# Cross-attention of a two-layer decoder: ScalarE's copies ahead of its newest exponential

## The chip, the cores and the metric

One core of a Trainium2 chip runs the whole program. Its engines are TensorE (PE, with PEld for its weight loads), VectorE (DVE), ScalarE (ACT), GpSimd (POOL) and SyncE (SP, which issues transfers). The time is device microseconds from start to end of one execution; the median of a few runs counts.

## What is computed

A decoder of two layers on x (4, 256, 256) with a context (4, 512, 64), all fp32. Each layer is self-attention, cross-attention and a mixture of experts, each followed by a layer norm of the sum with its input. The change touches cross-attention alone:

```
q_r    = rope((x @ Wq.T per head) @ w_kc_q) @ W_qr     # per head: 64 wide
k_r    = kv_r @ W_kr                                   # kv_r: the rotated context
attn   = softmax(q_r @ k_r.T)                          # 16 heads, 256 x 512 for each of 4 batches
ctx_c  = attn @ kv_r
out    = (ctx_c @ w_kc_kv, heads side by side) @ Wo.T
```

The kernel multiplies the weights together beforehand, so that scores are a query of 64 against the rotated context, and the context product is attn with the 64 columns of the rotated context.

## The kernel before

Cross-attention is cut into UNITS = 128 units per layer. Unit i is one tile of 128 queries of one head: scores of 128 x 512, their exponential, and the product with the context. Four units make a group g = i // 4 (one pair of heads, two query tiles). Every engine has a loop `cross_attention` of its own, written out by hand, over the same counter i; engines work their instructions in this order and meet through semaphores. In iteration i:

- TensorE (lines 654 to 694) makes the scores of unit i (two matmuls, L673 and L674, waiting until the score bank is free: `x_exp` of unit i - 3 in layer 0, which has three score banks, i - 4 in layer 1, which has four), then transposes the probabilities of unit i - 4 (L681, four transposes of 128 x 128 into bank 3 or 4, waiting for `x_nrm`, and for the copy of unit i - 6 out of that bank: `turned_probs_wait`), and, where i % 4 is 1, the context product of group i // 4 - 2 (L692, 16 matmuls).
- VectorE (lines 1147 to 1175) takes the negated row maximum of unit i (L1155, `x_max`), then the reciprocal of the sum of unit i - 2 (L1160, `x_rec`, after `x_exp`), and in layer 1 the copy of the transposed probabilities of an odd unit i - 4 (L1167, `x_tev_d`). In layer 0, for i up to 84, it also does one of five parts of the rounding of expert weights (lines 1171 to 1175).
- GpSimd (lines 1854 to 1862) multiplies the exponentials of unit i with the reciprocal (L1858, `x_nrm`); in layer 0, for i < 80, in iterations with i % 5 of 3 or 4 a part of that rounding (L1868, L1874) comes behind.
- ScalarE (lines 1641 to 1671) takes the exponential of unit i with its row sum (L1656, `x_exp`; a second small instruction reads the accumulator), waiting for `x_max` of unit i and `x_t` of unit i - 6; then copies the transposed probabilities of unit i - 4 out of bank 3 or 4 (L1664, `x_tev_a`), all units in layer 0, the even ones in layer 1; then, where i % 4 is 0, the context of group i // 4 - 3 (L1671, `x_ctx`).

Layer 0 runs as one loop over 128 units with the queries of the second half made in between at i = 64; layer 1 runs as two loops of 64 units. A loop goes on for some iterations behind its last unit, in which only the older units are worked.

Of the kernel before, what the change touches and what calls it, by code (L numbers as in the profile page):

```python
# [22 lines left out]
ACT = mybir.ActivationFunctionType  # L23
# [3 lines left out]
B, S, D = 4, 256, 256  # L27
# [5 lines left out]
NPAIR = H // 2  # L33
# [17 lines left out]
def program(nc, a, out):  # L51

    ctx = ExitStack()
    with ctx:
# [16 lines left out]
        ps = [ctx.enter_context(nc.psum_tensor(f"ps{i}", [P, 512], F32)) for i in range(8)]  # L71

        def sem(name):
            return ctx.enter_context(nc.semaphore(name))

        def at(kb, n, dt=F32, pattern=None, **k):

            words = n if dt != BF16 else n // 2
            v = mem[:, int(kb * 256):int(kb * 256) + words]
            v = v if dt == F32 else v.bitcast(dt)  # L80
            return v.rearrange(pattern, **k) if pattern else v
# [16 lines left out]
        PR = [at(kb, L) for kb in (80, 82, 84, 86, 200, 202)]  # L98
        SB = [[1, 2, 7], [0, 1, 2, 7]]
        CT = [at(kb, NPAIR * B * S, pattern="p (g s) -> p g s", g=NPAIR) for kb in (136, 136)]  # L100
# [5 lines left out]
        def col(n):  # L106
            cols[0] += n
            return small[:, cols[0] - n:cols[0]]
# [3 lines left out]
        nmax, esum, rinv = col(8), col(8), col(8)  # L112
# [36 lines left out]
        x_s, x_max, x_exp, x_nrm = sem("scores"), sem("neg_max"), sem("probs"), sem("probs_normed")  # L149
        x_rec, x_t, x_tev_a, x_tev_d = sem("sum_recip"), sem("probsT_psum"), sem("probsT_even"), sem("probsT_odd")  # L150
        x_pv, x_ctx = sem("context_psum"), sem("context_ready")
# [1437 lines left out]
        def _(act):  # L1589
# [44 lines left out]
            def high_queries(k, bank):  # L1634

                for hh in range(2):
                    r = slice(64 * hh, 64 * hh + 64)
                    last = act.activation(QS[2 * (k % NPAIR) + hh][r, :], ps[bank][r, :], ACT.Copy)  # L1638
                last.then_inc(x_qhi, 1)

            def cross_attention(lay, first, end):
                u0, g0 = UNITS * lay, UNITS // 4 * lay
                for i in range(first, end + 9):
                    if lay == 0 and i % (UNITS // 2) == 0 and i < end:
                        if i:
                            act.wait_ge(x_s, i)
                        for k in range(8 * (2 * i // UNITS), 8 * (2 * i // UNITS) + 8):
                            act.wait_ge(x_q, k + 1)
                            high_queries(k, SB[0][k % 3])
                        if i == 0:  # L1650
                            weights_copied(3, ps[3])
                    if i < end:
                        act.wait_ge(x_max, u0 + i + 1)
                        if i >= 6:
                            act.wait_ge(x_t, u0 + i - 5)
                        act.activation(PR[i % 6], ps[SB[lay][i % len(SB[lay])]][:, :], ACT.Exp, bias=nmax[:, i % 8:i % 8 + 1],  # L1656
                                       accum_out=esum[:, i % 8:i % 8 + 1]).then_inc(x_exp, 1)
                    j = i - 4
                    if first <= j < end and (lay == 0 or j % 2 == 0):
                        g = j // 4  # L1660
                        act.wait_ge(x_t, u0 + j + 1)
                        if g >= 2:
                            act.wait_ge(x_pv, g0 + g - 1)
                        act.activation(PT[g % 2][:, :, j % 2, (j // 2 % 2) * P:(j // 2 % 2 + 1) * P],  # L1664
                                       ps[3 + j % 2][:, :].rearrange("p (k s) -> p k s", k=KC), ACT.Copy)\
                           .then_inc(x_tev_a, 1)
                    g = i // 4 - 3
                    if i % 4 == 0 and first <= 4 * g:
                        b, p = g // NPAIR, g % NPAIR
                        act.wait_ge(x_pv, g0 + g + 1)  # L1670
                        act.activation(CT[lay][:, p, b * S:(b + 1) * S], ps[5 + g % 2][:, 0:S], ACT.Copy).then_inc(x_ctx, 1)  # L1671

            def weights_copied(f, bank):
                act.wait_ge(f_wt, f + 1)
                dst = w13T[:, :, f * 512:(f + 1) * 512] if f < 8 else w2T[:, :, (f - 8) * 512:(f - 7) * 512]
                act.activation(dst, bank[:, :].bitcast(BF16).rearrange("p (c n) -> p c n", c=DC), ACT.Copy).then_inc(f_wt_ev, 1)
# [127 lines left out]
            weights_copied(0, ps[1])  # L1804
            output_and_layernorm(0)
            cross_attention(0, 0, UNITS)
            output_and_layernorm(1)
            experts_layer0()
# [3 lines left out]
            for half in range(2):  # L1812
                narrow_queries(half)
                cross_attention(1, half * UNITS // 2, (half + 1) * UNITS // 2)
# [264 lines left out]
```

## Time and profile before

| | us |
|---|---|
| median of three runs (lowest, highest) | 1482.21 (1479.83, 1484.06) |
| the profiled execution | 1497.55 |
| its span, first to last instruction | 1495.7 |
| busy: PE, PEld | 1226.5, 830.7 |
| busy: DVE, ACT, POOL | 927.6, 592.9, 547.8 |

The profiled execution is longer than the timed ones; a difference in microseconds read from its trace is carried over to the median as it is. Cross-attention of layer 0 takes the span from about 121 to 360 us, that of layer 1 from about 882 to 984 and from about 1052 to 1155 us. "Idle before" in the profile is time in which an engine stood still ahead of an instruction, with the instruction that ended the wait; idle time on an engine that does not set the pace costs nothing.

### The profile page before, as it was taken

To read this page: it belongs to the slowest core of one execution; us is meant where nothing else is said; L and a number is where in the kernel's file an instruction comes from. 1 tells how busy PE (TensorE), PEld (TensorE's weight loads), DVE (VectorE), ACT (ScalarE), POOL (GpSimd) and SP (SyncE) were. 2 spreads that over 40 slices of the span, in tenths; PEclk is the share of its full clock that TensorE was granted. 3 is DMA by queue.
4 is the path that set the end of the run, shared out by engine and by line. 5 is a ranking of instruction groups with operands and counts; after the bars stand their busy time and mean duration, and the time that the engine had idled before them with its cause. 6 is when DMAs were issued, how large, how long until landed. Compare 5 with 4: busy or idle time off the path is not lost.

```text
span 1495.7 us, 22043 instructions
## 1 busy us (share of the span) xinstructions
PE 1226.5 (82%) x7024; PEld 830.7 (56%) x7024; DVE 927.6 (62%) x2269; ACT 592.9 (40%) x1524; POOL 547.8 (37%) x629
## 2 busy tenths in 40 slices
PE   7688888999849877689999989999899705988981
PEld 3555554666624365457677346643566604777770
DVE  1678786643597975839955876668665442444443
ACT  2247776774531102558810146621665121222220
POOL 2244673542242413525510014410343163444444
PEclk9899999999979978889997999999999957999996
DMA  7275993000001001010030000000400442554544
GB/s 278 77 224 167 305 313 116 1 1 1 29 1 42 1 1 71 3 54 2 2 120 0 0 0 1 1 1 1 197 1 30 188 154 74 85 81 79 82 70 105
DMA packets 69615, 110.75 MB, mean 74 GB/s; under 512 B 5056, under 2 KB 59840, under 8 KB 66240
## 3 DMA queue, kind: packets, MB, share of 16 engines
q1 hardware_dynamic: 58896, 96.62, 19.1%
q0 software_dynamic: 10608, 12.72, 5.9%
q8 instruction: 61, 1.00, 0.3%
q14 instruction: 50, 0.41, 0.1%
HBM read 57.41 MB, written 51.91 MB: 73 GB/s over the span
## 4 chain that ended last, share of the span: by engine, by line
PE 60%; DVE 17%; issue 8%; ACT 6%; DMA 4%; POOL 3%; another core or an unknown queue 1%; SPq 1%; POOLq 0%; DVEq 0%; ACTq 0%
PE ps L692 8%; PE ps L681 7%; PE ps L967 6%; PE ps L701 4%; PE ps L673 3%; PE ps L674 3%; PE ps L1021 2%; DMA sums<-mem 2%; ACT mem L1664 2%; PE ps L1018 2%; PE ps L948 2%; PE ps L641 2%; PE ps L803 2%; DVE mem L1155 1%; PE ps L786 1%
## 5 line engine op out<-in xcount | busy, mean ns | idle before, releaser
L1858 POOL TENSOR_SCALAR mem<-mem 128x512 f32<-128x512 f32 x256 | 178.3, 698 | 414.2 <-DVE mem L1160 411.3
L1155 DVE TENSOR_REDUCE mem<-ps 128x1 f32<-128x512 f32 x256 | 176.0, 688 | 132.4 <-PE ps L674 124.2
L1656 ACT ACTIVATE mem<-ps,mem 128x512 f32<-128x512 f32 x256 | 177.1, 692 | 123.6 <-DVE mem L1155 122.3
L681 PE MATMUL ps<-mem 128*128 128x128 f32 x1024 | 157.4, 277 | 35.4 <-ACT mem L1664 30.4
L681 PEld LDWEIGHTS ps<-mem 128*128 128x128 f32 x1024 | 120.5, 141 | 95.1 <-POOL mem L1858 67.6
L1924 POOL DMA_INDIRECT sums<-mem x63 | 97.1, 1541 | 131.6 <-DVE mem L1532 98.6
L673 PE MATMUL ps<-rounded_at 128*128 128x512 f32 x256 | 124.3, 486 | 11.7 <-DVE rounded_at L1144 10.4
L692 PE MATMUL ps<-mem 128*64 128x256 f32 x1024 | 124.8, 386 | 2.4 <-ACT mem L1664 2.4
L1664 ACT ACTIVATE mem<-ps 128x512 f32<-128x512 f32 x192 | 114.4, 597 | 6.3 <-PE ps L681 5.9
L1868 POOL TENSOR_TENSOR mem<-mem 128x512 f32<-128x512 f32 x40 | 55.4, 1384 | 139.2 <-DVE mem L1196 139.1
L1638 ACT ACTIVATE rounded_at<-ps 64x512 fp32r<-64x512 f32 x64 | 37.8, 591 | 166.3 <-PE ps L950 154.2
L674 PE MATMUL ps<-rounded_at 128*128 128x512 f32 x256 | 102.4, 400 | 0.0
L692 PEld LDWEIGHTS ps<-mem 128*64 128x64 f32 x1024 | 68.5, 137 | 40.8 <-issue 10.2
L1516 DVE TENSOR_TENSOR mem<-ps,mem 128x96 f32<-128x96 f32 x63 | 16.2, 257 | 117.5 <-ACT mem L1799 90.4
L967 PE MATMUL ps<-mem 128*128 128x512 f32 x192 | 86.0, 599 | 0.0
L1909 POOL TENSOR_TENSOR mem<-mem 128x512 f32<-128x512 f32 x48 | 49.9, 1040 | 62.5 <-DVE mem L1379 62.5
L1018 PE MATMUL ps<-mem 128*128 x252 | 55.7, 345 | 20.3 <-ACT mem L1790 17.3
L673 PEld LDWEIGHTS ps<-rounded_at 128*128 128x128 f32 x256 | 49.3, 193 | 38.7 <-ACT mem L1656 19.6
L1021 PE MATMUL ps<-mem 128*128 x252 | 67.1, 390 | 0.0
L1144 DVE TENSOR_TENSOR rounded_at<-ps,rounded_at 64x512 fp32r<-64x512 f32 x64 | 44.1, 689 | 34.2 <-ACT rounded_at L1638 33.7
L967 PEld LDWEIGHTS ps<-mem 128*128 128x128 f32 x192 | 35.3, 190 | 49.3 <-issue 39.1
L1799 ACT ACTIVATE mem<-ps 128x224 f32<-128x224 f32 x63 | 22.5, 357 | 101.3 <-PE ps L1021 101.3
(259 smaller groups left out, 2622.9 us busy)
## 6 DMA issues: line engine op xcount, KB each, us to landing
slots<-mem SPq DMA_DIRECT2D x15, 2312.0 KB, 10.0
mem<-in_f_w_dram SPq DMA_DIRECT2D x16, 1024.0 KB, 10.4
mem<-slots SPq DMA_DIRECT2D x63, 136.0 KB
mem<-in_f_w_dram SPq DMA_DIRECT2D x24, 256.0 KB, 3.4
mem<-in_x_wq_dram SPq DMA_DIRECT2D x2, 2048.0 KB, 13.2
mem<-in_x_wo_dram SPq DMA_DIRECT2D x2, 2048.0 KB, 8.5
mem<-sums SPq DMA_DIRECT2D x8, 256.0 KB, 4.5
mem<-in_x_wqr_dram SPq DMA_DIRECT2D x1, 1536.0 KB, 6.6
```

The lines of the kernel that those rows point to most:

```text
L673: pe.matmul(ps[sb[i % len(sb)]][:, :], q, KH[b], start=True, stop=False)
L674: pe.matmul(ps[sb[i % len(sb)]][:, :], q, KL[b], start=False, stop=True).then_inc(x_s, 1)
L681: mm = pe.transpose(ps[3 + j % 2][:, k * P:(k + 1) * P], PR[j % 6][:, k * P:(k + 1) * P], ident)
L692: mm = pe.matmul(ps[5 + g % 2][64 * hh:64 * hh + 64, 0:S], KV[:, b * KC + k, 0, :], PT[g % 2][:, k, hh, :], start=k == 0, stop=k == KC - 1)
L967: mm = pe.matmul(ps[SB[1][q % 4]][:, :], AQ[:, c, (3 * p + ch) * P:(3 * p + ch + 1) * P], XT[:, c, half * 512:(half + 1) * 512], start=c = ...
L1018: pe.matmul(both[:, :, 0:I1], xT1[:, i % 2, c, :], mem[:, bass.ds(at_large[i] + 2 * I1 * c, 2 * I1)], start=c == 0, stop=c == DC - 1)
L1021: mm = pe.matmul(both[:, :, I1:I1 + IC1], xT1[:, i % 2, c, :], mem[:, bass.ds(at_small[i] + 2 * IC1 * c, 2 * IC1)], start=c == 0, stop=c = ...
L1155: dve.tensor_reduce(nmax[:, i % 8:i % 8 + 1], ps[SB[lay][i % len(SB[lay])]][:, :], AX.X, ALU.max, negate=True)\
L1656: act.activation(PR[i % 6], ps[SB[lay][i % len(SB[lay])]][:, :], ACT.Exp, bias=nmax[:, i % 8:i % 8 + 1], accum_out=esum[:, i % 8:i % 8 + 1 ...
L1664: act.activation(PT[g % 2][:, :, j % 2, (j // 2 % 2) * P:(j // 2 % 2 + 1) * P], ps[3 + j % 2][:, :].rearrange("p (k s) -> p k s", k=KC), A ...
L1858: pool.tensor_scalar(PR[i % 6], PR[i % 6], rinv[:, i % 8:i % 8 + 1], 1.0, ALU.mult, ALU.mult)\
L1924: pool.indirect_dma_start(sums[i % 2], bass.IndirectOffsetOnAxis(ap=rows1[:, i % 8, IDX:IDX + 1].bitcast(U32), axis=0), y1[:, i % 4, :], N ...
```

## The change

ScalarE's loop works the same instructions with the same waits in another order within each iteration: the context copy first, then the copy of the transposed probabilities of unit i - 4, then the exponential of unit i. No instruction and no semaphore is added or removed, and the other engines' code is the same.

```
-                    if i < end:
-                        act.wait_ge(x_max, u0 + i + 1)
-                        if i >= 6:
-                            act.wait_ge(x_t, u0 + i - 5)
-                        act.activation(PR[i % 6], ps[SB[lay][i % len(SB[lay])]][:, :], ACT.Exp, bias=nmax[:, i % 8:i % 8 + 1],
-                                       accum_out=esum[:, i % 8:i % 8 + 1]).then_inc(x_exp, 1)
+                    g = i // 4 - 3
+                    if i % 4 == 0 and first <= 4 * g:
+                        b, p = g // NPAIR, g % NPAIR
+                        act.wait_ge(x_pv, g0 + g + 1)
+                        act.activation(CT[lay][:, p, b * S:(b + 1) * S], ps[5 + g % 2][:, 0:S], ACT.Copy).then_inc(x_ctx, 1)
                     j = i - 4
                     if first <= j < end and (lay == 0 or j % 2 == 0):
...
                            .then_inc(x_tev_a, 1)
-                    g = i // 4 - 3
-                    if i % 4 == 0 and first <= 4 * g:
-                        b, p = g // NPAIR, g % NPAIR
-                        act.wait_ge(x_pv, g0 + g + 1)
-                        act.activation(CT[lay][:, p, b * S:(b + 1) * S], ps[5 + g % 2][:, 0:S], ACT.Copy).then_inc(x_ctx, 1)
+                    if i < end:
+                        act.wait_ge(x_max, u0 + i + 1)
+                        if i >= 6:
+                            act.wait_ge(x_t, u0 + i - 5)
+                        act.activation(PR[i % 6], ps[SB[lay][i % len(SB[lay])]][:, :], ACT.Exp, bias=nmax[:, i % 8:i % 8 + 1],
+                                       accum_out=esum[:, i % 8:i % 8 + 1]).then_inc(x_exp, 1)
```

## Rows read from the trace of the kernel before

**Rows 1.** The page, part 5: costliest groups of instructions; idle before, and its releaser.
```profile
L1656 ACT ACTIVATE mem<-ps,mem 128x512 f32<-128x512 f32 x256 | 177.1, 692 | 123.6 <-DVE mem L1155 122.3
L681 PE MATMUL ps<-mem 128*128 128x128 f32 x1024 | 157.4, 277 | 35.4 <-ACT mem L1664 30.4
...
L1664 ACT ACTIVATE mem<-ps 128x512 f32<-128x512 f32 x192 | 114.4, 597 | 6.3 <-PE ps L681 5.9
```
**Rows 2.** Waits, 118 to 360 us: who waited for whom, us in total, times, longest.
```profile
PE ps L681 <- ACT mem L1664: 17.7, 45, 0.9
```
**Rows 3.** Waits, 877 to 983 us, the first half of layer 1.
```profile
PE ps L681 <- ACT mem L1664: 6.3, 15, 0.8
```
**Rows 4.** Chain that ended last, context products: start us, us, what.
```profile
276.54 1.88 PE ps L692 x16
...
347.97 1.88 PE ps L692 x16
...
891.95 1.88 PE ps L692 x16
...
973.04 1.88 PE ps L692 x16
```
**Rows 5.** Timeline of a group in layer 1: start us, us, engine, line, operation [idle before].
```profile
931.18 0.50 PE L673 MATMUL ps<-rounded_at 128*128 128x512 f32 x1
...
931.75 0.60 PE L681 MATMUL ps<-mem 128*128 128x128 f32 x4
931.95 0.69 DVE L1155 TENSOR_REDUCE mem<-ps 128x1 f32<-128x512 f32 x1 [1.63 <-PE ps L674]
...
932.67 0.69 ACT L1656 ACTIVATE mem<-ps,mem 128x512 f32<-128x512 f32 x1 [1.88 <-DVE mem L1155]
932.80 0.69 POOL L1858 TENSOR_SCALAR mem<-mem 128x512 f32<-128x512 f32 x1 [2.28 <-DVE mem L1160]
...
933.00 0.48 PE L673 MATMUL ps<-rounded_at 128*128 128x512 f32 x1
...
933.35 0.59 ACT L1664 ACTIVATE mem<-ps 128x512 f32<-128x512 f32 x1
...
933.70 0.69 POOL L1858 TENSOR_SCALAR mem<-mem 128x512 f32<-128x512 f32 x1 [0.20 <-DVE mem L1160]
...
934.09 0.63 PE L681 MATMUL ps<-mem 128*128 128x128 f32 x4 [0.38 <-ACT mem L1664]
...
934.47 0.47 PE L673 MATMUL ps<-rounded_at 128*128 128x512 f32 x1
...
935.01 0.60 PE L681 MATMUL ps<-mem 128*128 128x128 f32 x4
```
**Rows 6.** Timeline of a group in layer 0, units above 84.
```profile
325.43 0.69 POOL L1858 TENSOR_SCALAR mem<-mem 128x512 f32<-128x512 f32 x1 [2.55 <-DVE mem L1160]
...
326.34 0.69 POOL L1858 TENSOR_SCALAR mem<-mem 128x512 f32<-128x512 f32 x1 [0.21 <-DVE mem L1160]
...
326.71 0.63 PE L681 MATMUL ps<-mem 128*128 128x128 f32 x4 [0.37 <-ACT mem L1664]
...
327.12 0.60 ACT L1664 ACTIVATE mem<-ps 128x512 f32<-128x512 f32 x1
...
327.87 0.63 PE L681 MATMUL ps<-mem 128*128 128x128 f32 x4
```
**Rows 7.** Timeline of layer 0, units below 84, with the rounding: units 28 and 29.
```profile
172.87 1.27 POOL L1868 TENSOR_TENSOR mem<-mem 128x512 f32<-128x512 f32 x1
...
174.24 0.69 POOL L1858 TENSOR_SCALAR mem<-mem 128x512 f32<-128x512 f32 x1
...
174.99 0.66 PE L681 MATMUL ps<-mem 128*128 128x128 f32 x4 [0.50 <-POOL mem L1858]
```
**Rows 8.** Timeline of the same stretch, unit 37.
```profile
187.12 0.69 POOL L1858 TENSOR_SCALAR mem<-mem 128x512 f32<-128x512 f32 x1 [0.68 <-DVE mem L1160]
...
188.40 0.63 PE L681 MATMUL ps<-mem 128*128 128x128 f32 x4 [0.29 <-ACT mem L1664]
```

## The prediction

> **What bounds the kernel now.** I read the page first, then the waits of TensorE in the three stretches of cross-attention, then the chain that ended last, and last the timeline of single groups. The page shows ScalarE idle for 123.6 us ahead of its exponential, waiting for the row maximum, while TensorE's transposes are the group with the largest wait for ScalarE: 30.4 of their 35.4 us of idle time are put down to ScalarE's copy L1664 [rows 1]. The waits say where: 17.7 us in 45 waits in layer 0, 6.3 us in 15 waits in the first half of layer 1 [rows 2, 3]; the second half of layer 1 repeats the first, and the three sum to 30.3 us. The chain has every context product on it, so TensorE sets the pace, and it gives the period of a group of four units: (347.97 - 276.54) / 11 = 6.49 us in the part of layer 0 without the rounding, (973.04 - 891.95) / 13 = 6.24 us in layer 1 [rows 4].
>
> I call the units of a group by their number mod 4, in the order in which TensorE meets them: 2, 3, 0, 1, and behind 1 the context product. S2 is the scores of unit 2, T2 the transposes of the unit four earlier, and so on.
>
> **Layer 1, step by step** [rows 5]. S2 starts at 931.18, T2 at 931.75, done 0.60 later at 932.35. Its copy could run then: ScalarE has been idle for 1.88 us. But the exponential of unit 2 stands ahead of it and waits for the maximum (931.95 to 932.64), so it runs from 932.67 and the copy only from 933.35 to 933.94. T0 needs that copy (same bank) and starts at 934.09, with 0.38 us of wait. S1 follows 0.38 later, T1 0.54 behind S1, then the context product.
>
> With the copy first it runs from about 932.40 to 933.00 and T0 no longer waits for it. What is late next? Two things. TensorE itself: S0 starts at 933.00 and a transpose follows its scores by 0.54 (934.47 to 935.01), so 933.54. And GpSimd: its product for T0's unit runs from 932.80 to 933.49, and TensorE follows such a release by about 0.06 us (174.24 + 0.69 = 174.93, T at 174.99 [rows 7]), so 933.55. The two coincide; T0 comes 0.54 us earlier. Then S1 at 933.93 and T1 at 934.47; T1's unit leaves GpSimd at 933.70 + 0.69 = 934.39 [rows 5], plus 0.06 is 934.45, just in time. So nothing of the 0.54 is lost on the way to the context product. I take 0.52 us a group, bounded by the 0.38 that the row puts down to the copy and by 0.59, which is what is left if GpSimd never binds and T0 follows at the unstalled spacing.
>
> Number of such groups: 13 intervals between the context products [rows 4] and one ahead of the first product (15 waits in the half [rows 3]; the 15th lies behind the last scores, where the GpSimd product takes over). 14 x 2 halves x 0.52 = 14.6 us.
>
> **Layer 0 above unit 84** [rows 6]. All four copies are ScalarE's, and two waits fall in each group: T0 at 326.71 behind the copy of T2, and T1 at 327.87, 0.15 us behind the copy that runs from 327.12 to 327.72. With the copies first, T0 is held by GpSimd alone (325.43 + 0.69 + 0.06 = 326.18), S1 comes 0.38 later and T1 0.54 after that, 327.10, while GpSimd allows 326.34 + 0.69 + 0.06 = 327.09 and the second copy, which now runs about 326.2 to 326.8 behind the exponential of unit 2, allows 326.95. T1 comes 0.77 us earlier; I take 0.75, bounds 0.37 (only the wait named in the row goes) and 0.84. Eleven intervals between the two products of [rows 4] and the one behind them: 12 x 0.75 = 9.0 us.
>
> **Layer 0 below unit 84.** Here VectorE and GpSimd also round weights, in a pattern that repeats after 20 units, five groups. Where a rounding step lies between the two GpSimd products, T1 waits for GpSimd and not for ScalarE: L1868 from 172.87, the product at 174.24, T1 at 174.99 [rows 7]. By the positions of those steps (i % 5 of 3 or 4) that is so for two groups of five, and these gain nothing or next to nothing. In the others the wait is for ScalarE: GpSimd is done at 187.12 + 0.69 = 187.81, TensorE could go at 187.87 and goes at 188.40 [rows 8], so 0.53 us; a group behind a rounding step gets less of it. I take 0.26 us a group over 20 groups, 5.2 us; bounds 0 and 0.53, that is 0 to 10.6 us.
>
> **What the move costs ScalarE's other work.** The context copy goes ahead of two instructions in one iteration of four. It waits for a product that TensorE finished before S2, so it adds no wait, only its own 0.4 us. The exponential of unit 2 starts at about 932.9 instead of 932.67. Who waits for it? VectorE's reciprocal two iterations later, which comes behind the maximum of unit 0, about a microsecond after that exponential's end, and in layer 0 S1 through the score bank: the products at 932.80 [rows 5] and 325.43 [rows 6] are the same place of the group, 607.37 us apart, so T2 ends at 324.98 there, its copy runs to about 325.6, the exponential of unit 2 from about 325.5 to 326.3, and S1 comes at 326.56 in the new order. The exponential of unit 0 now stands behind the context copy, the copy and T0 and starts up to 0.3 us later; its reciprocal comes only behind the next group's S2. Each of these has cover, the thinnest about 0.2 us (S1 in layer 0); if it is gone it costs its shortage once a group. ScalarE's load in layer 0, 4 x (0.692 + 0.597) + about 0.4 = 5.6 us a group by the busy means [rows 1], overlapped in part, still fits into the new 5.74. In the first iterations, while the loops fill, the exponential of unit 4 is held behind T0's first copy by up to 0.7 us, but that of unit 5 waits for its maximum anyway: nothing. DMA queues are not moved past.
>
> **Sum.** 14.6 + 9.0 + 5.2 = 28.8 us off the profiled execution's 1497.55, so 1468.8. That execution is 15.3 us above the median of the runs shown, and the difference carries over: 1482.2 - 28.8 = 1453.4 us. By the bounds: 28 x 0.38 + 12 x 0.37 + 0 = 15.1 us at least and 28 x 0.59 + 12 x 0.84 + 10.6 = 37.2 us at most, 1467.1 to 1445.0.
>
> **Rivals.**
>
> *Another wait steps in at half the way.* GpSimd's product binds T0 within 0.01 us of TensorE's own pace [rows 5], so any delay there counts in full: if the later exponentials, or GpSimd beside a busier VectorE, push it by 0.25 us, layer 1 keeps 0.27 x 28 = 7.6, layer 0 0.5 x 12 = 6.0, the rounded part nothing: 13.6 us, 1468.6. For it: the coincidence. Against it: GpSimd was idle for 2.28 us before its product and 0.20 before the next [rows 5], and its input, the exponential of four iterations ago, is not near.
>
> *The exponential becomes the late one, and the kernel gets slower.* ScalarE stands at the transposes of unit i - 4 before it may take the exponential of unit i, and TensorE issues these behind the scores of unit i; with three score banks in layer 0, S of unit i + 3 waits for this exponential, and VectorE's reciprocal in both layers. It decides where the exponential ends after the point at which S1 stood before (T0 + 0.38 = 327.09), 0.8 us later than my timetable has it; a further 0.3 us on each of the 32 groups of layer 0, and 0.3 on 28 of layer 1 through the reciprocal, would be 18 us of loss, 1500. For it: ScalarE's load in layer 0 is the tightest after TensorE's. Against it: ScalarE is idle for 1.88 us in every group of layer 1 [rows 5] at just the place where the copy now goes. The Trainium skill, page "TensorE: Matmul & The Clock Gate", section "Architectural detail", states that ScalarE and VectorE are strict FIFO, while TensorE alone can pull weight loads ahead. By that rule a copy that waits holds the exponential behind it however ready that is, which is this rival; the trace agrees as far as it goes, since the ready copy of 932.35 stood until 933.35.
>
> *The move does nothing*: the waits put down to ScalarE were in truth GpSimd's. T0's start 0.15 us behind the copy's end and 0.60 behind GpSimd's speaks against it. It would leave 1482.
>
> **How the numbers follow.** Forecast 0.78, half-way rival 0.12, nothing 0.04, slower 0.05, and 0.01 for more than my bounds. About 0.3% (4.4 us) is what a measurement of this kernel can tell from no change. Faster: 0.78 + 0.12 + 0.01 = 0.91; same 0.04; slower 0.05. The range 1446 to 1468 holds the forecast with its bounds and most of the half-way case.
>
> **What would show it.** Right: TensorE's wait for L1664 falls from 30.4 us to a few; the period of the context products is about 5.72 us in layer 1 and 5.74 us above unit 84; groups with a GpSimd step between the products keep their length; ScalarE's idle time ahead of L1656 shrinks and some appears ahead of L1664, released by L681. Wrong: periods of 5.9 us or more with TensorE waiting for L1858 (half way), waits of L673 for L1656 of tenths of a microsecond in each group of layer 0 (slower), or unchanged T0 starts relative to S2, 2.91 us (nothing).

## The result and the profile after

The changed kernel took 1459.67 us, median of four runs (1457.3 to 1464.83), against 1483.13 us of the kernel before in four runs beside it: ratio 0.9847, interval 0.9813 to 0.9882, so 17 to 28 us faster. Run again later, six runs beside eleven of the kernel before, the ratio was 0.9798 (0.9762 to 0.9833). The forecast of 1453.4 was 6 us too low against the median of the first of the two: it had 28.8 us for the gain, and the two medians differ by 23.5. The profiled execution took 1464.83 us, its span 1463.0 us.

The page's costliest groups; lines 1663 and 1670 are now the copy of the transposed probabilities and the exponential.

```profile
L1670 ACT ACTIVATE mem<-ps,mem 128x512 f32<-128x512 f32 x256 | 177.1, 696 | 12.7 <-DVE mem L1155 12.1
L681 PE MATMUL ps<-mem 128*128 128x128 f32 x1024 | 159.0, 278 | 14.3 <-POOL mem L1858 13.4
...
L1663 ACT ACTIVATE mem<-ps 128x512 f32<-128x512 f32 x192 | 116.0, 606 | 93.2 <-PE ps L681 92.7
```

Against [rows 1]: busy times are the same within 2 us, and the waiting has changed its place. ScalarE's idle time ahead of the exponential went from 123.6 to 12.7 us, and 93.2 us now stand ahead of the copy (6.3 before), which waits there for TensorE's transposes. TensorE's transposes wait 14.3 us in place of 35.4, and no longer for ScalarE but for GpSimd.

The chain that ended last, context products (start us, us, what), answers to [rows 4]:

```profile
278.74 1.88 PE ps L692 x16
...
341.91 1.88 PE ps L692 x16
...
885.42 1.88 PE ps L692 x16
...
960.10 1.88 PE ps L692 x16
```

(341.91 - 278.74) / 11 = 5.74 us a group in layer 0 above unit 84, and (960.10 - 885.42) / 13 = 5.74 us in layer 1: 0.75 and 0.50 us less than before. The granted clock of TensorE is 1.00 in both traces from 280 to 345 and from 890 to 960 us, so it is not the clock. A group of layer 1 in the timeline (start us, us, engine, line, operation) shows why, beside [rows 5]:

```profile
910.78 0.60 PE L681 MATMUL ps<-mem 128*128 128x128 f32 x4
910.98 0.69 DVE L1155 TENSOR_REDUCE mem<-ps 128x1 f32<-128x512 f32 x1 [1.58 <-PE ps L674]
...
911.42 0.60 ACT L1663 ACTIVATE mem<-ps 128x512 f32<-128x512 f32 x1 [1.68 <-PE ps L681]
...
911.84 0.69 POOL L1858 TENSOR_SCALAR mem<-mem 128x512 f32<-128x512 f32 x1 [2.23 <-DVE mem L1160]
...
911.91 0.68 ACT L1670 ACTIVATE mem<-ps,mem 128x512 f32<-128x512 f32 x1
912.04 0.48 PE L673 MATMUL ps<-rounded_at 128*128 128x512 f32 x1
...
912.59 0.66 PE L681 MATMUL ps<-mem 128*128 128x128 f32 x4
...
912.74 0.69 POOL L1858 TENSOR_SCALAR mem<-mem 128x512 f32<-128x512 f32 x1 [0.21 <-DVE mem L1160]
913.00 0.48 PE L673 MATMUL ps<-rounded_at 128*128 128x512 f32 x1
...
913.55 0.60 PE L681 MATMUL ps<-mem 128*128 128x128 f32 x4
```

The copy starts 0.04 us behind the end of T2 (911.38), not 1.00 us. T0 starts at 912.59, 0.06 us behind the end of GpSimd's product (912.53): it is the late one now, as the forecast had it, by 0.01 us against TensorE's own pace (0.55 us behind S0 for 0.54). The start shows only part of its price: the four transposes of T0 take 0.66 us, where those of T1 take 0.60.

In layer 0 below unit 84 the step of GpSimd still stands between the two products, as in [rows 7], and this group takes 6.96 us before and 6.98 after:

```profile
171.14 1.28 POOL L1868 TENSOR_TENSOR mem<-mem 128x512 f32<-128x512 f32 x1
...
172.52 0.69 POOL L1858 TENSOR_SCALAR mem<-mem 128x512 f32<-128x512 f32 x1
...
173.26 0.66 PE L681 MATMUL ps<-mem 128*128 128x128 f32 x4 [0.94 <-POOL mem L1858]
```

Where did the time come from? Cross-attention of layer 0 ended at 360.10 before and 347.54 now, that of layer 1 at 1154.91 and 1129.30: 25.6 us in all. The two spans differ by 32.7. The other 7.1 us lie in the routing and the experts behind, which the change does not touch. The chain of the kernel before has the first of these pieces there, which this trace of the changed kernel lacks; but the second trace of the changed kernel has one too (the second piece), and so have the traces of all the experiments below:

```profile
1216.28 13.94 another core or an unknown queue
```
```profile
1185.09 12.49 another core or an unknown queue
```

So the missing piece is no effect of the change. From the end of layer 1's cross-attention to the end of the span it is 340.8 us before and 333.7 after, and between 331.4 and 344.6 over all twelve traces, in none of which that part of the program differs. A single pair of profiles would thus overstate the change. The 25.6 us of the stages lie inside both ratios' intervals (17 to 28 us and 25 to 36). In the second trace of the changed kernel the stages end at 346.05 and 1123.72, 31.2 us earlier in all, with the same periods of 5.74 to 5.75 us; the 5.6 us more lie outside the groups at their steady pace.

### The profile page after: what moved, and what is told of

The parts are those of the page before. It is cut to its first block, busy times and chain, and to the rows that moved or that the text cites. A ratio compares the mean times of both kernels' runs of the same rounds, so it can differ in the third digit from the quotient of the medians.

```text
span 1463.0 us, 22043 instructions
## 1 busy us (share of the span) xinstructions
PE 1228.0 (84%) x7024; PEld 833.0 (57%) x7024; DVE 924.3 (63%) x2269; ACT 590.8 (40%) x1524; POOL 547.2 (37%) x629
## 4 chain that ended last, share of the span: by engine, by line
PE 62%; DVE 18%; issue 6%; POOL 6%; DMA 4%; ACT 3%; SPq 0%; POOLq 0%; DVEq 0%; ACTq 0%
PE ps L692 8%; PE ps L681 6%; PE ps L967 6%; PE ps L701 4%; PE ps L673 4%; PE ps L674 3%; PE ps L1021 3%; PE ps L1018 3%; DMA sums<-mem 2%; PE ps L948 2%; PE ps L641 2%; PE ps L803 2%; POOL mem L1858 2%; DVE mem L1155 1%; PE ps L786 1%
## 5 line engine op out<-in xcount | busy, mean ns | idle before, releaser
L1670 ACT ACTIVATE mem<-ps,mem 128x512 f32<-128x512 f32 x256 | 177.1, 696 | 12.7 <-DVE mem L1155 12.1
L681 PE MATMUL ps<-mem 128*128 128x128 f32 x1024 | 159.0, 278 | 14.3 <-POOL mem L1858 13.4
L1663 ACT ACTIVATE mem<-ps 128x512 f32<-128x512 f32 x192 | 116.0, 606 | 93.2 <-PE ps L681 92.7
L1607 ACT ACTIVATE mem<-ps 128x256 f32<-128x256 f32 x40 | 15.3, 383 | 118.9 <-PE ps L454 118.9
```

Of the source, the lines that this page charges most:

```text
L681: mm = pe.transpose(ps[3 + j % 2][:, k * P:(k + 1) * P], PR[j % 6][:, k * P:(k + 1) * P], ident)
```

## The experiments

Each run is given with its ratio to runs of the kernel before beside it, and the interval of the ratio.

**Which of the two moved copies matters.** One kernel moves only the copy of the transposed probabilities (order: copy, exponential, context), one only the context copy (context, exponential, copy).

The orders in short (not the lines of the code, which calls no such functions):

```
before:  exponential(i); turned(i - 4); context(i // 4 - 3)
e1:      turned(i - 4); exponential(i); context(i // 4 - 3)
e2:      context(i // 4 - 3); exponential(i); turned(i - 4)
```

> Only the copy of the transposed probabilities goes ahead of the exponential; the context copy stays last. Theory A (the copy of T2 held behind the exponential is the whole loss): all of the gain is here, 22 to 28 us below the kernel before, periods of the context products 5.74 us in layer 1 and above unit 84 of layer 0, as with the whole change. Theory B (the context copy ahead takes part in it): less than 20 us, or periods off by 0.1 us or more. I expect A, with the ratio to before 0.980 to 0.986.

> Only the context copy goes ahead: context, exponential, copy of the transposed probabilities. Theory A: no gain, periods stay at 6.24 us (layer 1) and 6.49 us (layer 0 above unit 84), within 3 us of the kernel before; if anything a little longer in layer 0, because the copy of unit 0 still comes behind. Theory B: a gain of 3 us or more.

Measured: 0.9817 (0.9778 to 0.9856) for the first, 0.9990 (0.9965 to 1.0015) for the second. The chain of the first has the periods of the whole change, (340.03 - 282.57) / 10 = 5.75 us above unit 84 and (957.33 - 882.68) / 13 = 5.74 us in layer 1:

```profile
282.57 1.88 PE ps L692 x16
...
340.03 1.88 PE ps L692 x16
...
882.68 1.88 PE ps L692 x16
...
957.33 1.88 PE ps L692 x16
```

The page and the chain of the second show the old wait and the old period, (346.10 - 281.11) / 10 = 6.50 us:

```profile
L681 PE MATMUL ps<-mem 128*128 128x128 f32 x1024 | 155.7, 275 | 35.3 <-ACT mem L1669 29.2
```
```profile
281.11 1.88 PE ps L692 x16
...
346.10 1.88 PE ps L692 x16
```

All of the gain is in the copy of the transposed probabilities; the place of the context copy is worth nothing that can be measured. Theory B falls.

**Layer by layer.** The three parts of ScalarE's iteration become functions, and each layer takes them in its own order. The line of the first run; the second has `lay == 1`:

```
...
+                    order = (context, turned, exponential) if lay == 0 else (exponential, turned, context)
...
```

> The new order in layer 0 alone, layer 1 as before. By the stages of the two traces layer 0 gave 12.6 us (360.10 - 347.54) of the 26.4 us between them in cross-attention, so theory A expects 12 to 13 us, ratio about 0.992, and in the trace groups with a rounding step of GpSimd between two products unchanged in length. Rival C: the gain of layer 0 is given back behind it (the next stages grow); then less than 8 us in the time though the stage is 12.6 us shorter.

> The new order in layer 1 alone. Theory A: 28 groups of 0.50 us, 13 to 14 us, ratio about 0.991, and this with the run before adds up to the whole change (the two are independent). Rival C: 13.8 us shorter in the stage and less than 9 us in the time, because the experts behind it wait for transfers that did not start earlier.

Measured: layer 0 alone 0.9896 (0.9859 to 0.9932), layer 1 alone 0.9894 (0.9859 to 0.9929), some 15.5 us each with intervals of about 5 us to either side. Both lie above what was expected (12 to 13 and 13 to 14 us), and their sum is above the whole, but within the intervals. The chains of the two traces are sharper. Layer 0 alone (first context product and output projection of layer 0, then of layer 1):

```profile
140.32 1.88 PE ps L692 x16
...
352.24 10.56 PE ps L701 x48
...
884.05 1.88 PE ps L692 x16
...
1147.11 10.56 PE ps L701 x48
```

Layer 1 alone:

```profile
134.07 1.88 PE ps L692 x16
...
358.08 10.56 PE ps L701 x48
...
888.96 1.88 PE ps L692 x16
...
1138.51 10.56 PE ps L701 x48
```

With the new order layer 0 takes 211.9 us where it takes 224.0 with the old one, 12.1 less, and layer 1 takes 249.6 for 263.1, 13.5 less: 25.6 us together, about as for the whole. The stretch between the two layers is 531.8 us in the one and 530.9 in the other (531.9 before), and behind layer 1 it is 342.5 and 341.0 (340.8 before). So nothing is given back behind either stage, and rival C falls.

**What sets the period now.** VectorE's reciprocal of unit i - 2 is put ahead of the maximum of unit i, once on top of the change and once on the old order of ScalarE. GpSimd's product then comes earlier.

```
+                    r = i - 2
+                    if first <= r < end:
+                        dve.wait_ge(x_exp, u0 + r + 1)
+                        dve.reciprocal(rinv[:, r % 8:r % 8 + 1], esum[:, r % 8:r % 8 + 1]).then_inc(x_rec, 1)
                     if i < end:
                         dve.wait_ge(x_s, u0 + i + 1)
...
-                    r = i - 2
...
```

> The whole change, and VectorE takes the reciprocal of unit i - 2 ahead of the maximum of unit i, so that GpSimd's product comes earlier. Theory D (after the change GpSimd's product is the late one for T0, and in the groups with rounding for T1): the period falls from 5.74 to about 5.65 us above unit 84 and in layer 1 (39 groups, 3 to 4 us), and the groups below unit 84 fall from a mean of 6.5 to 5.8 to 6.1 us (20 groups, 8 to 14 us); in all 37 to 44 us below the kernel before, ratio 0.971 to 0.976. Theory E (TensorE's own work sets 5.74, and VectorE's load the groups below 84): periods unchanged, within 3 us of the whole change.

> The kernel before with only VectorE's reciprocal ahead of the maximum, ScalarE's order as it was. If before the change ScalarE's copy was the late one (theory A), GpSimd being earlier gives nothing in layer 1 and above unit 84 (6.24 and 6.49 us), and at most 3 us in the groups with a rounding step between the products. If GpSimd was in truth the bound there, periods fall by 0.1 us or more.

Measured on top of the change: 0.9739 (0.9696 to 0.9782). Its page and its chain (above unit 84, and in layer 1):

```profile
L681 PE MATMUL ps<-mem 128*128 128x128 f32 x1024 | 155.1, 275 | 7.4 <-POOL mem L1858 5.4
```
```profile
275.81 1.88 PE ps L692 x16
...
326.85 1.88 PE ps L692 x16
...
873.02 1.88 PE ps L692 x16
...
941.10 1.88 PE ps L692 x16
```

(326.85 - 275.81) / 9 = 5.67 us and (941.10 - 873.02) / 12 = 5.67 us: the 0.07 us a group that GpSimd held TensorE back. On the old order, against the kernel before: 0.9988 (0.9958 to 1.0017); TensorE's waits in the first half of layer 1 hardly differ from [rows 3], and the period above unit 84 is (344.32 - 279.32) / 10 = 6.50 us:

```profile
PE ps L681 <- ACT mem L1664: 6.2, 15, 0.8
```
```profile
279.32 1.88 PE ps L692 x16
...
344.32 1.88 PE ps L692 x16
```

So the same edit is worth nothing that can be measured before the change, and some 9 to 16 us behind it (0.9739 against 0.9798 and 0.9847 of the change, each against other runs of the kernel before, so this is rough). The traces are sharper again: without the change the edit leaves the periods of 6.50 and 6.24 us as they were and only shortens the 13 intervals of layer 0 before unit 64 from 88.6 to 87.0 us (by the starts of the context products in the timeline, here and below). This shows both halves of the story: before, ScalarE's copy was late and not GpSimd; after, GpSimd is. The groups below unit 84 came out short of what was expected: the stage from the first product to the projection takes 338.02 - 133.13 = 204.9 us against 347.54 - 134.32 = 213.2, of which some 0.8 us belong to the groups above, so 7.5 us and not 8 to 14; and the mean of the 13 intervals before unit 64 fell from 6.53 to 6.21 us, not to between 5.8 and 6.1.

**How near the slower rival was.** In layer 0 the exponential of the unit with i % 4 of 2 is taken twice, first into a spare buffer, so that the counted one ends later.

```
+                        if lay == 0 and i % 4 == 2:
+                            act.activation(at(168, L), ps[SB[lay][i % len(SB[lay])]][:, :], ACT.Exp, bias=nmax[:, i % 8:i % 8 + 1])
```

> The whole change, and in layer 0 the exponential of every unit with i % 4 of 2 is taken twice (the first into a spare buffer), which makes the counted one end some 0.6 us later. This tests how near the slower rival was. In the trace of the changed kernel that exponential ends 0.3 us ahead of the scores of unit 1, which wait for its bank. So I expect TensorE to wait 0.3 to 0.45 us for it in each group above unit 84 (period 6.0 to 6.2 us, 4 to 5 us in all), less below unit 84 where GpSimd binds, and layer 1 unchanged; together 4 to 9 us above the changed kernel. If the exponentials had the 0.8 us of slack of my timetable, nothing.

Measured: 0.9834 (0.9778 to 0.9890). This lies between the two ratios of the changed kernel, 0.9798 and 0.9847, so the time alone shows no loss; the trace does. Above unit 84 the weight load of S1 waits some 0.3 us for the exponential in every group, where the changed kernel's does not wait at all. The waits from 130 to 340 us (3.1 us in 8 waits in the changed kernel), the counted exponential with S1 behind it, and the chain:

```profile
PEld ps L673 <- ACT mem L1672: 9.7, 34, 0.4
```
```profile
312.72 0.69 ACT L1672 ACTIVATE mem<-ps,mem 128x512 f32<-128x512 f32 x1
...
313.55 0.19 PEld L673 LDWEIGHTS ps<-rounded_at 128*128 128x128 f32 x1 [0.31 <-ACT mem L1672]
313.56 0.50 PE L673 MATMUL ps<-rounded_at 128*128 128x512 f32 x1
```
```profile
284.15 1.88 PE ps L692 x16
...
345.37 1.88 PE ps L692 x16
```

The period above unit 84 is (345.37 - 284.15) / 10 = 6.12 us, 0.38 more than the changed kernel's, 4.3 us in all. Below unit 84 nothing is lost (84.9 us for the 13 intervals in both traces), nor in layer 1. The counted exponential starts 2.27 us behind S2 where it starts 1.70 behind in the changed kernel: a delay of 0.57 us costs 0.38 us a group, so its slack was about 0.2 us. The rival's mechanism is real and its margin thin, since this exponential is what the change itself pushes back, by 0.2 us: before, it starts 1.50 us behind S2.

**The rounding out of the way.** It is spread over 8 units an item instead of 5, GpSimd's steps behind the products of units with i % 4 of 3, VectorE's parts outside the iteration with i % 4 of 2.

```
...
-                        k, part = EARLY8 + i // 5, i % 5
-                        if k < NW8 and part < 3:
-                            exponents(k, raww[k % 3], part)
-                        if EARLY8 < k <= NW8 and part >= 3:
-                            clipped(k - 1, rndw[(k - 1) % 4], late8[k - 1 - EARLY8], part - 3)
+                        k, r = EARLY8 + i // 8, i % 8
+                        if k < NW8 and r in (0, 1, 4):
+                            exponents(k, raww[k % 3], (0, 1, 4).index(r))
+                        if EARLY8 < k <= NW8 and r in (3, 5) or i == end + 3:
+                            for part in (0, 1) if i == end + 3 else ((3, 5).index(r),):
+                                clipped(k - 1, rndw[(k - 1) % 4], late8[k - 1 - EARLY8], part)
...
-                    k, part = EARLY8 + i // 5, i % 5
-                    if lay == 0 and k < NW8 and part >= 3:
-                        rounded(k, raww[k % 3], expw[k % 2], rndw[k % 4], part - 3)
+                    k, r = EARLY8 + i // 8, i % 8
+                    if lay == 0 and r % 4 == 3:
+                        rounded(k, raww[k % 3], expw[k % 2], rndw[k % 4], r // 4)
```

> The whole change, and the rounding of the expert weights in layer 0 is spread over 8 units an item instead of 5: GpSimd's two steps stand behind the product of units with i % 4 of 3, which is when TensorE is in the context product, and VectorE's five parts avoid the iteration with i % 4 of 2. Theory D: no rounding step is between the products that T0 and T1 wait for, so all groups of layer 0 run at 5.74 to 5.9 us: 20 groups from 6.5, less some that VectorE's parts cost above unit 84, 10 to 15 us below the changed kernel, ratio to before 0.972 to 0.977. Theory E (VectorE's load itself): the work per unit is only thinned, the groups run at 6.0 to 6.2 throughout and the gain is under 5 us.

Measured: 0.9740 (0.9692 to 0.9788). The chain in the first half of layer 0 gives (209.27 - 139.08) / 12 = 5.85 us, where the changed kernel needs a mean of 6.5:

```profile
139.08 1.88 PE ps L692 x16
...
209.27 1.88 PE ps L692 x16
```

Theory E, which had 6.0 to 6.2 us, falls. The price is that the rounding now goes on above unit 84, where the groups take 5.85 us too instead of 5.74. The work is the same in all, and what it costs has fallen: 0.79 us a group above the pace of 5.74 for the 20 groups with rounding, against 0.11 us for all 32 now. The total amount of the work is thus not what kept these groups long. Whether it was the place of GpSimd's steps alone or also their number in a group (two in five units before, one in four now) this run does not separate, since it changes both.

**Both additions**, and the changed kernel once more beside them.

> The whole change with both additions: VectorE's reciprocal ahead of the maximum, and the rounding spread over 8 units an item. Theory D: with GpSimd's product early and its rounding steps off the way, TensorE alone sets layer 0: periods of 5.65 to 5.75 us in all of it (5.85 with the rounding moved alone), 5.67 in layer 1; 4 to 5 us below the rounding moved alone in layer 0 and 2 us in layer 1, ratio to before 0.966 to 0.972. Theory F (VectorE's in-order wait for the exponentials, which the reciprocal first brings forward, collides with its rounding parts): layer 0 stays at 5.8 or more, ratio 0.972 to 0.976.

> The changed kernel as it is, again, in the same call as the version with both additions, for a closer ratio. The stages of cross-attention in the trace give 26.4 us, so I expect 0.980 to 0.984.

Measured: 0.9668 (0.9637 to 0.9698) with both, 1443.3 us against 1493.9, and 0.9798 (0.9762 to 0.9833) for the change alone, 1459.9. The page and the chain of the first (both parts of layer 0, layer 1):

```profile
L681 PE MATMUL ps<-mem 128*128 128x128 f32 x1024 | 154.3, 274 | 2.5 <-DVE mem L1167 1.0
```
```profile
137.41 1.88 PE ps L692 x16
...
205.56 1.88 PE ps L692 x16
...
248.51 1.88 PE ps L692 x16
...
316.66 1.88 PE ps L692 x16
...
863.02 1.88 PE ps L692 x16
...
925.47 1.88 PE ps L692 x16
```

The change alone came out just below the 0.980 to 0.984 that was expected of it. Periods of (205.56 - 137.41) / 12 = 5.68, (316.66 - 248.51) / 12 = 5.68 and (925.47 - 863.02) / 11 = 5.68 us: the same everywhere, and TensorE's transposes wait 2.5 us in the whole kernel. TensorE's own work sets the stage. Theory F falls. From the first to the last context product layer 0 takes 194.2 us for the 197.7 with the rounding moved alone, 3.4 less where 4 to 5 were expected. This version beats both kernels.

## Why the prediction was right

- *The copy of T2 held behind the exponential is the loss.* Right, and shown from three sides: the whole gain with this copy alone, none with the context copy, none with an earlier GpSimd.
- *Layer 1: 28 groups of 0.52 us.* Measured 6.24 - 5.74 = 0.50, so 13.9 us for 14.6.
- *Layer 0 above unit 84: 12 x 0.75 us.* The period fell by 0.75 us (6.49 to 5.74) over 11 intervals, 8.3 us. The twelfth interval I had counted here still has rounding in it and gave about half a microsecond (6.50 to 6.03 by the starts of its two products, 276.46 and 282.96 before, 272.64 and 278.67 after). 8.7 us for 9.0.
- *Below unit 84: 20 x 0.26 us.* 3.8 us for 5.2: the product at 276.46 came at 272.64. The size was a guess between 0 and 0.53 from two groups, and by the traces it was a good one: the five groups of the pattern take 6.97, 6.67, 6.72, 6.66 and 7.13 us before and 6.97, 6.25, 6.22, 6.16 and 7.02 after, 0.31 us a group, with two that gain nothing or 0.11, as foreseen. What falls short is the stretch at unit 64, where the queries of the second half are made: from the last product ahead of it to the second behind it the time is 33.0 us before and 34.1 after. The second trace of the changed kernel has 32.8 there, and the runs above that leave VectorE and GpSimd as they are have 31.2 to 33.4, so this is spread and not a cost of the change. In that second trace the product comes at 271.11, 5.35 us earlier than before, for the 5.2.
- *What is late next.* GpSimd's product for T0, foreseen to 0.01 us. That nothing of it would reach the period was too simple: with GpSimd's product early the period is 0.07 us shorter, 5.67 for 5.74. The upper bounds of 0.59 and 0.84 stand for a group of 5.65 us, which is near that.
- *The exponential's cover of about 0.2 us in layer 0.* Right by the run that delays it. The rival's text counts its loss from where S1 stood before, 0.8 us behind the timetable, while the paragraph on ScalarE's other work has 0.2 us for the same cover. Both hold: behind 0.2 us part of the gain goes, behind 0.8 us the kernel would be slower than before.
- *The range.* The half-way rival's 1468.6 lies just outside the 1446 to 1468 that was said to hold most of it. The outcome did not come near enough for this to matter.
- *The sum.* 28.8 us for 25.6 in the two stages of the trace. About 0.8 us of the miss is a stretch between them that grew (360.10 to 753.78 before, 347.54 to 741.97 after, 393.7 and 394.4 us); the second trace of the changed kernel has 393.8 there, so this too is spread. The rest is the terms above: 26.4 us for 28.8.

What stays open: why layer 0 alone and layer 1 alone each came out at 15.5 us in time, when their traces have 12.1 and 13.5 us in the stages; the intervals allow that it is chance.

## What to carry to other kernels

In a software pipeline written out by hand, an engine that works in order should take the older unit's work first when its input is ready at a time at which the newer unit's is not: the idle time ahead of the newest instruction (1.88 us here) was the place for the copy that TensorE waited for. After such a move look for what is late next and by how much, since an edit that is worth nothing before it (the reciprocal) may be worth something behind it. Auxiliary work put in by a count of its own (every 5 units in groups of 4) sooner or later falls between the two instructions that must not be parted; giving it a period that fits the groups, and fewer steps in each, brought these from 6.5 to 5.85 us, and the groups that had none from 5.74 to 5.85. And look at more than one trace before a difference outside the changed stage is given a cause.

## What the runs showed of the hardware

TensorE followed a release by GpSimd within 0.06 us (912.53 to 912.59) and by ScalarE within 0.15 us (933.94 to 934.09 [rows 5]); ScalarE followed TensorE's transposes within 0.04 us (911.38 to 911.42). These are differences of ends and starts as the profile gives them, and the same 0.15 us stands in layer 0 (327.72 to 327.87 [rows 6]); a timetable to a hundredth of a microsecond needs the pair's own row. ScalarE took its instructions in the order of the program: the copy whose input was ready at 932.35 stood until 933.35 behind the exponential [rows 5]. The medians of the kernel before differed from one set of runs to another by up to 13 us (1482.2, 1495.1, 1492.1, 1493.9), half of what was to be measured, so each version is compared with the runs of the kernel before beside it.
